# A two-block gated layer: the moves of an alignment path are found on GpSimd instead of VectorE

## What is computed

```python
def _L0_xattn_ref(teacher_features, student_features):     # ctx_1024, layernorm(x)
    def _align_one(small, large):                          # 1500 rows, 56 rows
        D = _pairwise_euclidean(small, large)
        R = _dtw_cost(D)          # R[i,j] = D[i,j] + min(R[i-1,j], R[i,j-1], R[i-1,j-1])
        i_idx, j_idx, valid = _backtrack(R, T_small, T_large)
        contrib = small[i_idx] * valid[:, None]
        return zeros.at[j_idx].add(contrib)                # rows of the context, summed along the path
    return jax.vmap(_align_one)(teacher_features, student_features)

x = x + tanh(g_xattn[0]) * _L0_xattn_ref(ctx_1024, layernorm(x))
x = x + tanh(g_ffn[0])   * _L0_ffn_ref(layernorm(x), ...)       # one of 8192 experts by product keys
x = x + tanh(g_xattn[1]) * _L1_xattn_ref(layernorm(x), ctx_1024, ctx_1024, ...)   # 16 heads
x = x + tanh(g_ffn[1])   * _L1_ffn_ref(layernorm(x), ...)       # 8 experts, two taken
return x
```

## Time and profile before

| | |
|---|---|
| median of 3 runs | 522.02 us (520.3 to 523.67) |
| the profiled execution | 522.08 us |
| its span in the trace | 520.3 us |
| the 70 steps of the table | from 24.9 us to 119.3 us of the span |
| the hops back | from 123.2 us to 173 us |

### The profile page before, as it was taken

How to read it: one execution, slowest core, us unless ns; L and a number is a source line. 1 busy time by engine, 2 the same in 40 slices (tenths; PEclk the granted TensorE clock), 3 DMA queues, 4 the chain that set the end, 5 groups by cost and what they waited for, 6 DMA issues and landing times.

```text
span 520.3 us, 10115 instructions
## 1 busy us (share of the span) xinstructions
PE 423.9 (81%) x4010; PEld 253.7 (49%) x4010; DVE 372.8 (72%) x978; ACT 254.0 (49%) x438; POOL 64.5 (12%) x99
## 2 busy tenths in 40 slices
PE   8998877758888888100778899999999999889996
PEld 5444343436655574000234466666666666544443
DVE  7759999997666785866686888988988982371222
ACT  3565877553322691100103456666666666634443
POOL 1000000001000001777330000120110121000000
PEclk9999999896999999655999999999999999999999
DMA  8600664243413103993171005375375390000000
GB/s 283 237 0 24 208 200 147 97 134 110 152 59 86 36 1 70 205 234 95 47 160 24 0 3 132 72 157 122 71 169 117 72 316 4 1 1 0 1 1 18
DMA packets 28941, 50.28 MB, mean 97 GB/s; under 512 B 2470, under 2 KB 18622, under 8 KB 28894
## 3 DMA queue, kind: packets, MB, share of 16 engines
q1 hardware_dynamic: 27070, 45.96, 32.7%
q0 software_dynamic: 1536, 3.67, 2.8%
q10 hardware_dynamic: 288, 0.00, 0.0%
HBM read 39.96 MB, written 9.45 MB: 95 GB/s over the span
## 4 chain that ended last, share of the span: by engine, by line
PE 47%; DVE 34%; issue 7%; POOL 7%; ACT 3%; DMA 2%; DVEq 0%; POOLq 0%; ACTq 0%
PE banks L1589 7%; PE banks L1565 7%; POOL arena L551 6%; PE banks L1620 5%; DVE work L1225 4%; DVE mx L1004 4%; PE banks L1667 4%; DVE arena L1194 4%; PE banks L1681 4%; DVE arena L1249 2%; DVE mx L1012 2%; PE banks L1282 2%; PE banks L1433 2%; DVE work L1189 2%; PE banks L1286 2%
## 5 line engine op out<-in xcount | busy, mean ns | idle before, releaser
L1004 DVE TENSOR_REDUCE mx<-banks 112x1 f32<-112x500 f32 x168 | 107.1, 676 | 16.4 <-PE banks L1565 16.4
L759 ACT ACTIVATE arena<-banks 128x896 f32<-128x896 f32 x96 | 87.9, 917 | 48.4 <-PE banks L1620 47.7
L1304 PE MATMUL banks<-steps,one 128*128 128x500 f16 (+1 forms) x201 | 55.1, 368 | 33.3 <-DVE hcol L952 33.3
L1589 PE MATMUL banks<-arena 128*32 128x112 f32 (+1 forms) x1536 | 57.1, 265 | 1.5 <-ACT arena L759 0.9
L1565 PE MATMUL banks<-ctxT,arena 96*112 96x500 bf16 x144 | 54.7, 393 | 3.8 <-DVE mx L1004 1.1
L1589 PEld LDWEIGHTS banks<-arena 128*32 128x32 f32 (+1 forms) x1536 | 33.7, 109 | 21.5 <-issue 18.9
L1304 PEld LDWEIGHTS banks<-steps,one 128*128 128x128 f16 x201 | 20.2, 102 | 47.7 <-issue 37.0
L1225 DVE SCALAR_TENSOR_TENSOR work<-twice,banks,arena 128x202 f32<-128x202 f32 x68 | 29.5, 434 | 18.9 <-PE banks L1433 18.9
L1620 PEld LDWEIGHTS banks<-arena,ctxT 99*128 99x128 bf16 (+1 forms) x576 | 37.5, 103 | 10.2 <-issue 2.4
L1620 PE MATMUL banks<-arena,ctxT 99*128 99x112 bf16 (+1 forms) x576 | 41.2, 213 | 0.3 <-issue 0.3
L637 ACT ACTIVATE arena<-banks,wts 128x375 bf16<-128x375 f32 x64 | 33.9, 599 | 9.6 <-PE banks L1351 9.6
(11 more groups left out here) (262 smaller groups left out, 718.0 us busy)
## 6 DMA issues: line engine op xcount, KB each, us to landing
ctxT<-key_parts SPq DMA_DIRECT2D x36, 375.0 KB, 7.1
key_parts<-arena SPq DMA_DIRECT2D x32, 281.2 KB, 3.2
ctxT<-in_ctx_T SPq DMA_DIRECT2D x12, 500.0 KB, 8.8
arena<-key_parts SPq DMA_DIRECT2D x12, 375.0 KB, 7.5
ctxT<-in_ctx_nat SPq DMA_DIRECT2D x5, 750.0 KB
arena<-in_ctx_nat SPq DMA_DIRECT2D x3, 750.0 KB
arena<-in_L_ffn_W SPq DMA_DIRECT2D x1, 2048.0 KB, 9.8
arena<-in_fold_w SPq DMA_DIRECT2D x1, 768.0 KB, 5.6
```

The lines of the kernel that those rows point to most:

```text
L759: nc.scalar.activation(Pt[0:rows, g % 2, :].rearrange("p (a n) -> p a n", a=2), banks[0:rows, 2 + 2 * (g % 2):4 + 2 * (g % 2), 0:HQ // 2], ...
L1004: nc.vector.tensor_reduce(mx3[:, b % 2, u // NPIECE, u % NPIECE:u % NPIECE + 1], ps[k % 2][0:2 * NJ, 0:PIECE], AX_X, ALU.max).then_inc(s_m ...
L1304: nc.tensor.matmul(bank[:, 0:cols], one16[:, :], steps16[:, 0:cols], start=True, stop=True, skip_group_check=True)
L1589: last = nc.tensor.matmul(ps[6 + b % 2][q:q + 32, o:o + 2 * NJ], vals[0:rows, v0:v0 + 32], Pt[0:rows, g % 2, 2 * t * NJ:2 * (t + 1) * NJ], ...
```

## The change

For the first twelve pieces (`SIDE`) the two comparisons leave DVE. POOL takes two differences of 500 elements into a row of 1000 float32 (`gaps`), then compares the whole row with zero into float16 marks (`moves`). DVE waits for the differences (`s_gap`) before it writes over the ring of `m`. The last three pieces of marks stay on DVE, under a semaphore of their own (`s_nvl`). The key pieces of the chunks are spread 3, 2, 3, 3, 2, ... instead of seven 3s and five 2s. Five small table instructions of DVE move from after step 9 to between two distance pieces before step 5, and distance piece 10 moves from before step 5 to before step 6.

```diff
-    KEYS_OF_CHUNK = [0, 1] + 7 * [3] + 5 * [2]
+    KEYS_OF_CHUNK = [0, 1] + [3, 2, 3, 3, 2, 3, 2, 3, 3, 2, 3, 2]
+    SIDE = NTB - 2
-        left = [work[:, 6 * N_B + a * N_B // 2:6 * N_B + (a + 1) * N_B // 2].bitcast(F16) for a in range(2)]
...
+        moves = [work[:, (6 + a) * N_B:(7 + a) * N_B].bitcast(F16) for a in range(2)]
+        left = [m[:, 0:N_B] for m in moves]
+        never = [m[:, N_B:2 * N_B] for m in moves]
+        gaps = work[:, 4 * N_B:6 * N_B]
...
-            sp.wait_ge(s_nv, NCODES)
+            sp.wait_ge(s_nv, SIDE)
+            sp.wait_ge(s_nvl, NCODES - SIDE)
             sp.dma_start(foldw, fold_w[:, :]).then_inc(s_wqT, 16)
...
             done2(nc.gpsimd.tensor_scalar(mku[:, :], mk2[:, :], -1.0, 1.0, ALU.mult, ALU.add))
+            for k in range(SIDE):
+                pool.wait_ge(s_scan, CODES[k][0] + TB)
+                if k >= 1:
+                    pool.wait_ge(s_nv, k)
+                t, n = CODES[k]
+                nc.gpsimd.tensor_tensor(three(gaps[:, 0:N_B]), R_slot(t, n, 1, C), R_slot(t, n, 0, C), ALU.subtract)
+                nc.gpsimd.tensor_tensor(three(gaps[:, N_B:2 * N_B]), R_slot(t + 1, n, 0, C),
+                                        three(mring[:, t % (2 * TB) * C:(t % (2 * TB) + n) * C]), ALU.subtract
+                                        ).then_inc(s_gap, 1)
+                pool.wait_ge(s_gap, k + 1)
+                if k >= 2:
+                    pool.wait_ge(s_code, k - 1)
+                nc.gpsimd.tensor_scalar(moves[k % 2][:, :], gaps, 0.0, None, ALU.is_lt).then_inc(s_nv, 1)
             pool.wait_ge(s_dt, NTB)
...
-            D2_AT = {1: (6,), 3: (7,), 5: (8, 9, 10), 8: (11,)}
+            def spare_tables():
+                link(nc.vector.tensor_scalar(lane_i[:, :], pidx[:, :], DH, None, ALU.bitwise_and))
...
+            D2_AT = {1: (6,), 3: (7,), 5: (8, 9), 6: (10,), 8: (11,)}
             for t in range(STEPS):
                 for u in D2_AT.get(t, ()):
                     d2_of(u)
+                    if u == 8:
+                        spare_tables()
                 m = mring[:, (t % (2 * TB)) * C:(t % (2 * TB) + 1) * C]
                 if t >= 1:
                     ve.wait_ge(s_scan, t)
+                if t % TB == 0 and t >= 2 * TB:
+                    ve.wait_ge(s_gap, min(t // TB - 1, SIDE))
...
-                if t == 2 * TB - 1:
-                    ve.wait_ge(s_scan, t + 1)
-                    jump_inputs(0)
...
-                if t % TB == 1 and t >= 2 * TB:
-                    jump_inputs(t // TB - 1)
+                if t == SIDE * TB + TB + 1:
+                    ve.wait_ge(s_code, SIDE - 1)
+                    moves_of(SIDE)
                 if t == STEPS - 2:
                     ve.wait_ge(s_scan, t + 1)
                     ve.wait_ge(s_code, NTB - 2)
-                    jump_inputs(NTB - 1)
+                    moves_of(NTB - 1)
                 if t % TB == 4 and t >= 2 * TB:
                     jump_targets(t // TB - 2)
...
             def jump_codes(k):
-                pe.wait_ge(s_nv, k + 1)
+                pe.wait_ge(s_nv if k < SIDE else s_nvl, k + 1 if k < SIDE else k + 1 - SIDE)
```

More of the change, by code:

```diff
@@ L144, in build_gated_layers @@
         dts = work[:, 2 * N_B:4 * N_B]
-        left = [work[:, 6 * N_B + a * N_B // 2:6 * N_B + (a + 1) * N_B // 2].bitcast(F16) for a in range(2)]
-        o_nv = 8 * N_B + KQW
-        never = [w.bitcast(F16) for w in (work[:, 7 * N_B + N_B // 2:8 * N_B], work[:, o_nv:o_nv + N_B // 2])]
-        assert o_nv + N_B // 2 <= 10 * N_B
+        moves = [work[:, (6 + a) * N_B:(7 + a) * N_B].bitcast(F16) for a in range(2)]
+        left = [m[:, 0:N_B] for m in moves]
+        never = [m[:, N_B:2 * N_B] for m in moves]
+        gaps = work[:, 4 * N_B:6 * N_B]
         gate = work[:, 10 * N_B:]
@@ L326, in build_gated_layers @@
         s_scan = sem("column_scanned")
+        s_gap = sem("moves_compared")
+        s_nvl = sem("last_not_left_marks_ready")
         s_nv = sem("rows_not_left_ready")
@@ L421, in build_gated_layers @@
         R_slot = lambda k, n, lo, cnt: view(R[:, :], [[SLOT, n], [1, cnt]], k * SLOT + lo)
+        three = lambda a: a.rearrange("p (t c) -> p t c", c=C)
         block = ctx.enter_context(nc.Block())
@@ L1163, in _, with moves_of @@
             shift = [LB - 1] + list(range(LB - 1)) + [2 * LB - 1] + list(range(LB, 2 * LB - 1))
-            three = lambda a: a.rearrange("p (t c) -> p t c", c=C)
-            def jump_inputs(k):
+            def moves_of(k):
                 t, n = CODES[k]
@@ L1172, in jump_inputs @@
                                         three(mring[:, t % (2 * TB) * C:(t % (2 * TB) + n) * C]), ALU.is_lt
-                                        ).then_inc(s_nv, 1)
+                                        ).then_inc(s_nvl, 1)
             def jump_targets(k):
@@ L1180, in jump_targets @@
                                              ps[3 - k % 2][:, 0:n * SLOT], 0.0, ALU.add, ALU.max).then_inc(s_carry, 1)
-            D2_AT = {1: (6,), 3: (7,), 5: (8, 9, 10), 8: (11,)}
+            def spare_tables():
+                link(nc.vector.tensor_scalar(lane_i[:, :], pidx[:, :], DH, None, ALU.bitwise_and))
+                nc.vector.tensor_scalar(rowc21[:, :], rowc2[:, :], 1.0, None, ALU.add)
+                link(nc.vector.tensor_copy(hm[:, 0:1], lane_i[:, :]))
+                link(nc.vector.tensor_scalar(hm[:, 1:2], hm[:, 0:1], 0.0, None, ALU.is_gt))
+                link(nc.vector.tensor_scalar(hm[:, 0:1], hm[:, 1:2], 0.0, None, ALU.is_equal))
+            D2_AT = {1: (6,), 3: (7,), 5: (8, 9), 6: (10,), 8: (11,)}
             for t in range(STEPS):
@@ L1213, in _ @@
             ve.wait_ge(s_scan, STEPS)
-            jump_inputs(NTB)
+            moves_of(NTB)
             for k in range(NTB - 2, NCODES):
```

## The result

The changed kernel takes 523.21 us (median of 20 runs, 521.2 to 524.97), the kernel before 521.58 (20 runs): a ratio of 1.0031, with a 95% interval from 1.0017 to 1.0046. So it is slower by 1.6 us, a difference that 20 runs can tell from none and that is well within one per cent. The forecast was 529 us, 7 us slower.

What follows compares the result with a forecast made beforehand. DVE was taken to set the pace over the 70 steps, except at the start. From 522.08 us, ten chunks at +0.75 (+7.5) and 0.7 gained at the start gave 528.9, say 529 us; range 510 to 539.

Steps and rivals of the forecast that it cites:

- the price of a chunk: Ten full chunks, pieces 2 to 11: DVE 1.80 us late against 1.05 gained, +0.75 us each, +7.5 us together.
- The freed time: DVE's steps: each of the twelve pieces whose two comparisons leave DVE frees 1.05 us.
- A difference takes 1.24 us: POOL, each chunk: a difference of 500 elements takes 0.19 us plus 2.1 ns per further element, 1.24 us.
- the rival of quick differences: POOL's differences take 1.02 us each; lateness 0, 0.62 and 0.76 us, 0.33 us a chunk, 525 us; chance 0.14.
- The hand-over 0.14 us before the end: Between POOL and DVE: whichever begins first keeps the other out until 0.14 us before its recorded end.
- A comparison takes 1.07 us: POOL, each chunk: comparing 1000 elements takes 1.07 us, upper end 2.3; DVE's second minimum comes 0.76 us late.
- The rival of a slow comparison: POOL's comparison takes 2.3 us, second minimum 1.2 us later: 1.95 us a chunk, 541 us; chance 0.12.
- The order, minimum before second difference: Chunk start: DVE's waiting first minimum goes before POOL's second difference, coming in 0.20 us late.
- the rival's: POOL takes both differences in one go; first minimum 1.38 us late, 1.12 us a chunk, 533 us; chance 0.12.
- The start: Up to about 58 us: moved tables and distance piece 10 gain 1.2 us; 0.7 gained after piece 1's holds.
- What costs nothing: Key-piece spread, PE's wait for POOL's marks, DVE's wait for differences, and work behind POOL's 36 instructions add no time.
- No hindrance: DVE's minimum and scan slip beside POOL's instructions: chunks of 5.1 us, 10.2 us gained, 512 us; chance 0.20.

Runs made afterwards that it cites:

- The copy of 1.02 us: The changed kernel with POOL's comparison replaced by a copy of the 1000 float32 onto themselves, marks left out: 523.96 us, ratio 1.0042.
- the old list: The changed kernel with the earlier spread of key pieces, seven 3s and then five 2s: 523.79 us, 1.0047 to the kernel before.
- the memset run: The changed kernel with POOL's two differences and comparison replaced by memsets of the same outputs, marks of twelve pieces left out: 508.52 us, ratio 0.9777.

## Why the prediction was wrong

The mechanism was the forecast's: DVE is kept out by what POOL reads, and the steps named as late are those that are late, but for one. The sizes were off: the price of a chunk was put at 0.75 us and is 0.36, that of the start at a gain of 0.7 and is 1.2. Ten chunks and the start make 10 x 0.36 - 1.2 = 2.4 us, which is the 2.2 of the trace but for the 0.24 of the last targets; 6.8 were forecast. Most of the miss, 3.9 us, lies in the ten chunks.

- *The freed time, 1.05 us a chunk:* right. The chunk without POOL's reads shows 1.03.
- *A difference takes 1.24 us:* this is the term that failed. The first takes 1.02 us, the second 1.20 with the wait behind the first minimum in it. The rate of 2.1 ns came from L582, an instruction of 224 elements; the better row was L577 in the earlier trace rows, with 448 nearer in length, at 1.66 ns, which the forecast kept for the rival of quick differences. Why an element of L582 costs more, no run shows. With 1.02 the first difference has given the way free when the first minimum comes, which is then not 0.20 us late but on time, and the scan is 0.71 late instead of 0.84. That rival came nearest: it had 0.33 us a chunk and 525 us.
- *The hand-over 0.14 us before the end:* rough. In the chunk shown the scan comes in at 64.39 - 0.43 = 63.96, which is 0.20 before the second difference's recorded end at 64.16; and that difference ends 1.02 us after the end of the minimum at 63.14, not 1.02 after a point 0.14 before it. This is why the scan is 0.71 late and not the 0.62 of the rival.
- *A comparison takes 1.07 us and keeps the minimum out for nearly all of that:* wrong in the length, right in the price, and that by luck. It takes 2.71 us, more than the upper end of 2.3. But the step "whichever begins first keeps the other out until 0.14 us before its end" holds only where reading seems to fill the instruction. The copy of 1.02 us does hold until 0.14 before its end; the comparison lets go 1.84 before its own. The minimum is 0.70 late where 0.76 was forecast; by the forecast's own step the true length would have made it 0.70 + 1.70 = 2.40. The rival of a slow comparison saw the length and priced it as a hold to the end, at 541 us; it missed by 18.
- *The order, minimum before second difference:* right here. The first minimum is on time where the rival's would have been 1.38 us late, and the second difference takes 0.20 longer than the first, the time from its start at 62.94 to the minimum's end at 63.14.
- *The Trainium skill's sentence (SBUF — State Buffer, SBUF: two separate sides) that the one that starts first keeps the other out for the whole instruction:* the runs here differ for the instruction with a constant, and nearly agree for the copy; the hold was 0.46, 0.87 and 0.88 us for 500, 1000 and 1000 elements read, whatever the instruction's 1.46, 2.71 and 1.02.
- *The start:* the 1.2 us of tables and piece 10 came as worked out, and the run with them alone shows them. Piece 1's holds were put at 1.56 us and are 0.34 + 0.71, so its price just cancels the 1.05 that its comparisons free.
- *What costs nothing:* the key spread, shown by the old list. That the waits for the differences and the marks cost nothing is shown by the changed kernel's own rows, where the targets and the first minimum follow as closely as before.
- *No hindrance, 512 us, chunks of 5.1:* its condition is given only in the memset run, with 508.5 us and chunks of 5.14. Its chunks were right and its time 3.5 us too long, mostly because it gave only 0.8 us to the steps up to the scan of step 20. That scan starts 57.98 - 24.92 = 33.06 us after step 0 in the kernel before and 54.82 - 24.44 = 30.38 in the memset run, a gain of 2.68.

With 1.02 us for a difference and a hold of 0.87 us for the 1000 elements, the placing of the prediction gives 0, 0.62 and 0.70 us, or 1.32 - 1.03 = 0.29 us a chunk. The measured 0, 0.71 and 0.70 give 1.41 - 1.03 = 0.38, and the chunk shows 0.36. So the two sizes, the difference's above all, bring the forecast's 0.75 down to 0.29, and the hand-over most of the way back to 0.36.

## What to carry to other kernels

Work that moves from DVE to POOL is not free when it reads SBUF: lay its reads beside the DVE instructions and count those with two SBUF inputs. Give DVE's chain an input from PSUM where one is there already; here that turned a loss of 0.3% into a gain of 1%, and ACT lost a copy. And when two rows of the same operation give different rates, take the one nearer in length: here 448 elements gave the right time for 500, and 224 did not.

## What was not expected of the hardware

POOL's instruction with a constant (comparison or multiplication, to float16 or float32) takes 2.71 us for 1000 float32 and 1.46 for 500, 2.5 ns an element, while a copy of the same 1000 takes 1.02. In all of these DVE is kept out for 0.8 to 0.9 ns an element read, probably as long as the reading takes, and not for the rest; memsets, which read nothing, don't keep it out at all. A scan of 100 elements takes 0.42 us with its distances in PSUM and 0.43 with them in SBUF.
